# A fused attention and feed-forward kernel: first-pass scores by single PSUM banks, a new order of products, another ending

## The chip, the cores and the metric

The kernel runs on one core of one Trainium2 chip. The metric is the device time of one execution in microseconds (us). Engines are called by the profile's names: PE (TensorE matmul) with PEld (its weight loads), DVE (VectorE), ACT (ScalarE), POOL (GpSimd) and SP (SyncE, which here only issues DMAs). Each runs its own queue in order, and they meet through semaphores.

## The reference

Four sequences of 1024 tokens with 256 features. Every token is normalised, and the result goes through an attention layer (16 query heads, 2 key heads, 16 features a head, rotary positions) and, beside it, through a gated feed-forward layer with a Walsh-Hadamard transform. Both results are added to x.

```python
xn = layernorm(x)
q, k, v = xn @ wq + bq, xn @ wk + bk, xn @ wv + bv     # 16, 2 and 2 heads of 16
q, k = rotate(q) * 16 ** -0.5, rotate(k)
attn = softmax(q @ k.T * 16 ** -0.5)                    # 1024 x 1024 for each head
a = (attn @ v) @ wo + bo
h = fwht(silu(xn @ W1.T) * (xn @ W3.T))                 # 1024 wide
out = x + a + h @ W2.T
```

## The kernel before

**Stages.** There are `NIT` = 8 iterations, one for each sequence and key head, and each has `PERIODS` = 16 periods. Iteration i also carries the feed-forward work of token block i (512 tokens, 8 blocks) and prepares the projections of block i + 2. Products of float32 quality are made of three products of rounded parts (`TERMS`).

**Two passes over the scores.** The exponentials need the row maxima first. The first pass ("S1", one of 64 `UNITS` for each half of an iteration's heads) makes scores with queries on the partitions: two products of 48 rows, which lie in the two row halves of PE (rows 0 to 63 and 64 to 127) and go to the two banks of a slot. DVE takes the maximum over both banks with one `tensor_reduce` of 128x1024 (`unit`, L1295), and the two halves can run in PE side by side. The maxima are turned by DVE, placed by SP among the query rows (`place_maxima`) and so enter the second pass. The second pass (`score`, L1545) makes scores with keys on the partitions, one head into one bank; three banks (4 to 6) take turns, and ACT reads each with an exponential (L1079). `sums` (L1558) multiplies the exponentials by the values into bank 7; a step has four heads, and the trace has eight PE records for it. A period has four units of the first pass, four calls of `scores` (each of two heads, again in the two row halves) and two steps of `sums`.

**The slots.** Banks 0 to 3 are two slots of two banks in the iterations (slots 2 and 3 share banks 4 to 7 and serve the opening). Every entry into a slot waits on `ring_free` until the former entry has been read in full, and its reader waits on `ring_full`. `ring_table` counts these at build time; `PIECES`, `FULLS` and `FREES` say how many pieces, fills and readings an entry has. A unit is one piece, one fill and one reading. The entries of slot 0 are mostly the period's own work: `UP` (eight a block: gate and linear products, 24 products of 512 columns in four pieces, read by ACT's `gate` and `linear` and DVE's `gated`, L1267), `DN` (four a block, 48 products of 256 columns, read by `down`), `WO` (the output projection of a half, read by `projected_sums`), `XT`, `QK`, `Q2` and `VT` (turned tokens, projections and values of block i + 2). First-pass units use slot 1 and, where slot 0 has time, slot 0.

**The order** is written out by hand. `walk_iteration` calls, for each kind of period, `scores`, `first` (a unit), `own` (pieces of the period's entry), `sums_before` (the step left from the period before) and `sums` in the order in which PE has them. `kind_of` names the kind: with a trailing "o" where ACT also copies bank 7 (`save_sums`), `None` where a period has no entry. `LEAD` = 24 units run ahead of the second pass. ACT and DVE have orders of their own for each kind.

**The end.** After the last step of `sums`, `select` moves numerators and denominators of the last heads by two products with a selecting matrix; DVE makes reciprocals of 64x256 and multiplies, and PE makes the output projection of both halves; the last block leaves from ACT's DMA queue.

## Time and profile before

| | us |
|---|---|
| median of 3 runs | 1079.11 (1078.23 to 1080.97) |
| the profiled execution | 1075.6 |
| its span, first to last instruction | 1073.8 |
| PE busy, share of the span | 1014.3, 94% |
| DVE busy | 771.2, 72% |
| ACT busy | 707.5, 66% |
| POOL busy | 347.2, 32% |

The profiled execution lies 3.5 us below the median. A busy PE record reaches from the start of a product to its modelled end, and records overlap: two products that follow each other closely have starts .23 us apart and last .39 us each. So the distance of starts tells how fast PE works, and the busy share tells little about it.

### The profile page before, as it was taken

To read this page: it belongs to the slowest core of one execution; us is meant where nothing else is said; L and a number is where in the kernel's file an instruction comes from. 1 tells how busy PE (TensorE), PEld (TensorE's weight loads), DVE (VectorE), ACT (ScalarE), POOL (GpSimd) and SP (SyncE) were. 2 spreads that over 40 slices of the span, in tenths; PEclk is the share of its full clock that TensorE was granted. 3 is DMA by queue.
4 is the path that set the end of the run, shared out by engine and by line. 5 is a ranking of instruction groups with operands and counts; after the bars stand their busy time and mean duration, and the time that the engine had idled before them with its cause. 6 is when DMAs were issued, how large, how long until landed. Compare 5 with 4: busy or idle time off the path is not lost.

```text
span 1073.8 us, 19578 instructions
## 1 busy us (share of the span) xinstructions
PE 1014.3 (94%) x7604; PEld 549.6 (51%) x7604; DVE 771.2 (72%) x934; ACT 707.5 (66%) x1336; POOL 347.2 (32%) x300
## 2 busy tenths in 40 slices
PE   4889999999999999999999999999999999999997
PEld 3554445545554555545554455545555454644454
DVE  5996688677776778767786777767776778776723
ACT  4256677657765777657776577667775678566873
POOL 5262722073312634054310735126320224012300
PEclk9998999999999999999999999999999999999999
DMA  8762155212052253402242250521123131510001
GB/s 234 177 172 75 53 137 104 74 57 86 17 117 78 76 136 66 100 21 84 64 103 74 97 126 18 117 64 51 51 62 71 33 83 33 111 32 6 12 8 50
DMA packets 64941, 84.03 MB, mean 78 GB/s; under 512 B 19960, under 2 KB 34168, under 8 KB 64848
## 3 DMA queue, kind: packets, MB, share of 16 engines
q1 hardware_dynamic: 63296, 80.74, 29.1%
q10 hardware_dynamic: 1552, 2.03, 0.7%
q8 instruction: 60, 0.98, 0.4%
q14 instruction: 33, 0.27, 0.1%
HBM read 54.97 MB, written 22.51 MB: 72 GB/s over the span
## 4 chain that ended last, share of the span: by engine, by line
PE 66%; DVE 17%; ACT 5%; issue 4%; DMA 4%; SPq 3%; POOL 2%; DVEq 0%; ACTq 0%; POOLq 0%
PE ps L1501 16%; PE ps L1558 14%; PE ps L1545 13%; DVE negpart L1295 11%; PE ps L1456 9%; PE ps L1513 8%; PE ps L1467 3%; DVE hid L1267 3%; PE ps L1434 3%; ACT work L1079 2%; DMA qk_parts<-hid 1%; DMA xn<-in_x 1%; SPq L776 1%; SPq L784 1%; DMA recip_rows<-dens 1%
## 5 line engine op out<-in xcount | busy, mean ns | idle before, releaser
L1295 DVE TENSOR_REDUCE negpart<-ps 128x2 f32<-128x1024 f32 x512 | 619.0, 1224 | 235.7 <-PE ps L1456 234.8
L1079 ACT ACTIVATE work<-ps 128x512 f32<-128x512 f32 x1024 | 560.0, 603 | 262.3 <-PE ps L1545 256.9
L1558 PE MATMUL ps<-work,vb 128*32 128x512 f32 x2048 | 274.6, 609 | 5.8 <-ACT osum L1090 5.0
L1545 PE MATMUL ps<-qh,kb 50*128 50x512 f32 x1024 | 265.1, 450 | 10.3 <-ACT work L1079 7.4
L1456 PE MATMUL ps<-kb,qh 48*128 48x512 f32 x1024 | 226.8, 433 | 9.6 <-DVE negpart L1295 5.3
L1545 PEld LDWEIGHTS ps<-qh,kb 50*128 50x128 f32 x1024 | 123.4, 185 | 212.3 <-ACT work L1079 159.0
L1501 PE MATMUL ps<-xf,w_p 64*128 64x512 f32 x1536 | 218.3, 400 | 7.4 <-DVE negpart L1295 1.4
L1501 PEld LDWEIGHTS ps<-xf,w_p 64*128 64x128 f32 x1536 | 143.6, 185 | 49.7 <-DVE hid L1267 16.3
L933 POOL TENSOR_TENSOR hid_p<-hid,hid_p 128x512 fp32r<-128x512 f32 x64 | 82.2, 1286 | 203.1 <-ACT hid_p L1068 203.1
L1456 PEld LDWEIGHTS ps<-kb,qh 48*128 48x128 f32 x1024 | 98.1, 185 | 82.7 <-DVE negpart L1295 48.4
L1513 PEld LDWEIGHTS ps<-w2t_p,hid_p 64*128 64x128 f32 x1536 | 107.7, 185 | 34.2 <-DVE negpart L1295 27.1
L929 POOL TENSOR_TENSOR hid<-hid 128x512 f32<-128x512 f32 x60 | 77.3, 1288 | 136.1 <-DVE hid L1267 119.1
L1513 PE MATMUL ps<-w2t_p,hid_p 64*128 64x256 f32 x1536 | 116.8, 282 | 2.0
L952 POOL TENSOR_TENSOR attnt<-attnt,recips 128x512 f32<-128x512 f32 x15 | 19.3, 1285 | 282.0 <-DMA recips<-recip_rows 282.0
L1558 PEld LDWEIGHTS ps<-work,vb 128*32 128x32 f32 x2048 | 40.8, 108 | 83.1 <-issue 57.4
L1267 DVE SCALAR_TENSOR_TENSOR hid<-hid,ps 128x512 f32<-128x512 f32 x60 | 40.7, 678 | 5.2 <-ACT hid L1058 5.2
L1068 ACT CAST hid_p<-hid 128x512 fp32r<-128x512 f32 x64 | 40.0, 627 | 0.7 <-POOL hid L929 0.7
L1064 ACT COPY hid<-ps 128x512 f32<-128x512 f32 x60 | 37.1, 618 | 2.2 <-PE ps L1501 2.2
L1434 PE MATMUL ps<-xt,wqkv_p 128*128 128x512 f32 x126 | 36.7, 430 | 1.8 <-DVE xt L1260 1.4
L1467 PE MATMUL ps<-wo_sb,attnt 128*128 128x256 f32 x128 | 36.1, 415 | 1.5 <-DVE attnt L1422 0.9
L1058 ACT ACTIVATE hid<-ps 128x512 f32<-128x512 f32 x60 | 36.7, 611 | 1.2 <-PE ps L1501 0.3
L1275 DVE TENSOR_TENSOR y<-y,ps 128x256 f32<-128x256 f32 x32 | 13.2, 412 | 26.9 <-PE ps L1513 26.9
(125 smaller groups left out, 484.6 us busy)
## 6 DMA issues: line engine op xcount, KB each, us to landing
xf<-xn_parts SPq DMA_DIRECT2D x32, 512.0 KB, 8.5
qh<-qk_parts SPq DMA_DIRECT2D x192, 64.0 KB, 2.3
xn_parts<-xt SPq DMA_DIRECT2D x14, 512.0 KB, 3.5
qh<-mturned SPq DMA_DIRECT2D x256, 2.0 KB
y<-in_x SPq DMA_DIRECT2D x8, 512.0 KB, 4.8
attnt<-osum SPq DMA_DIRECT2D x124, 32.0 KB, 2.0
recips<-recip_rows SPq DMA_DIRECT2D x120, 32.0 KB, 1.8
xn<-in_x SPq DMA_DIRECT2D x7, 512.0 KB, 5.0
```

What stands on the lines that cost most here:

```text
L929: nc.gpsimd.tensor_tensor(hid[1][:, c, :], hid[1][:, c, :], hid[0][:, c, :], ALU.mult).then_inc(hid_done, 1)
L933: nc.gpsimd.tensor_tensor(hid_p[1][:, c, :], hid[1][:, c, :], hid_p[0][:, c, :].bitcast(F32), ALU.subtract).then_inc(hid_lo, 1)
L1079: nc.scalar.activation(prob[(ITSTEPS * i + j) % NPROB][:, h, :], ps[:, 4 + u % 3, :], ACT.Exp, scale=SCALE).then_inc(exp_done, 1)
L1267: nc.vector.scalar_tensor_tensor(at, at, 1.0, two(slot)[:, 0, :], ALU.add, ALU.mult).then_inc(ring_free[slot], 1)
L1295: nc.vector.tensor_reduce(negpart[a][:, f, :, h, t, e], two(slot), AX.X, ALU.max, negate=True).then_inc(ring_free[slot], 1)
L1434: m = pe.matmul(out, left[a], right[b], start=(first and n == 0), stop=(last and n == 2))
L1456: m = pe.matmul(bank[:, r, :], qh[2 * q + f][rows, h, t * P:(t + 1) * P], kb[i % 2][rows, e * 512:(e + 1) * 512], start=True, stop=True)
L1467: m = pe.matmul(bank[:, k // 2, k % 2 * D:(k % 2 + 1) * D], attnt[:, f, k * P:(k + 1) * P], wo_sb[:, i % NG, :], start=True, stop=True)
L1501: m = pe.matmul(bank[:, r, :], w13_p[w][rows, k, c * P:(c + 1) * P], xf[v][rows, k, :], start=(k == 0 and t == 0), stop=(done and t == 2))
L1513: m = pe.matmul(bank[:, r, 0:D], hid_p[w][rows, c, at * P:(at + 1) * P], w2t_p[v][rows, c, :], start=(c == 0 and t == 0), stop=(c == HC - ...
L1545: pe.matmul(ps[:, 4 + u % 3, :], kb[i % 2][rows, kt * P:(kt + 1) * P], qh[2 * a + f][rows, h, :], start=True, stop=True).then_inc(s2_done, 1)
L1558: m = pe.matmul(ps[VW * h:VW * (h + 1), 7, :], vb[b % 2][g][:, kt, :], prob[(ITSTEPS * i + j) % NPROB][:, h, :], start=(kt == 0), stop=(kt ...
```

## The change

1. **Units in two pieces.** `PIECES["S1"]`, `FULLS["S1"]` and `FREES["S1"]` become 2. A piece is one product into one bank, first of the upper row half (bank r = 1), then of the lower. DVE reduces each bank with an instruction of its own (128x512) when that bank is full. Where a unit follows a unit in its slot, a piece waits only until its own bank has been read (`RING[entry][3]`).
2. **A new order.** All kinds in `walk_iteration` are rewritten with `first(slot, n, ...)`, which places single halves; scores or own pieces stand between the two halves of a unit. ACT's order is adapted.
3. **SP's queue.** `load_turned(i + 1)` and `load_queries(i + 1, 1, 0)` now stand behind `spread_recips(i, 0)` and `place_maxima(i + 1, 0, 0)`.
4. **The end.** In the last iteration the four `DN` entries move one period ahead (11 to 14), the last `UP` to period 9, and `WO` of the first half gets period 15 (kind `WOz`). `select` is replaced by `last_values`: DVE turns bank 7 in blocks of 32x32, takes reciprocals of 128x8, multiplies, turns back, and PE adds its products with `wo_last` (rows of `wo` spread out, loaded in iteration 6) to products of the heads that were ready. The two halves of the last addition are 128x512 each as before; the 128x1024 addition is in period 15.
5. **The opening.** In `weights2` two more products stand behind the wait for the stored queries; the kinds `Nos` and `Not` of the first two periods are rewritten too.

In iteration 3, a period of kind `UP` away from ACT's copies, PE's queue before (L1501 is `UP`, L1456 a unit, L1545 scores, L1558 sums):

```order
L1501 MATMUL ps<-xf,w_p 128x512 x12
L1456 MATMUL ps<-kb,qh 128x512 x2
L1545 MATMUL ps<-qh,kb 128x512 x2
L1558 MATMUL ps<-work,vb_1 32x512 x4
L1545 MATMUL ps<-qh,kb 128x512 x2
L1456 MATMUL ps<-kb,qh 128x512 x2
L1501 MATMUL ps<-xf,w_p 128x512 x6
```

The same place after (L1538 is `UP`, L1495 a half of a unit, L1582 scores, L1595 sums):

```order
L1538 MATMUL ps<-xf,w_p 128x512 x6
L1495 MATMUL ps<-kb,qh 128x512
L1538 MATMUL ps<-xf,w_p 128x512 x6
L1495 MATMUL ps<-kb,qh 128x512
L1582 MATMUL ps<-qh,kb 128x512 x2
L1595 MATMUL ps<-work,vb_1 32x512 x4
L1495 MATMUL ps<-kb,qh 128x512
L1582 MATMUL ps<-qh,kb 128x512 x2
L1495 MATMUL ps<-kb,qh 128x512
L1538 MATMUL ps<-xf,w_p 128x512 x12
```

A unit's two products, which stood together, now have six `UP` products or two scores between them.

In iteration 7, period 4 (kind `WOo`), PE's queue before (L1467 is `WO`):

```order
L1558 MATMUL ps<-work,vb_1 32x512 x4
L1456 MATMUL ps<-kb,qh 128x512 x4
L1545 MATMUL ps<-qh,kb 128x512 x4
L1467 MATMUL ps<-wo_sb,attnt 128x256 x4
L1545 MATMUL ps<-qh,kb 128x512 x2
L1558 MATMUL ps<-work,vb_1 32x512 x4
```

and after (L1504 is `WO`):

```order
L1495 MATMUL ps<-kb,qh 128x512
L1582 MATMUL ps<-qh,kb 128x512 x2
L1495 MATMUL ps<-kb,qh 128x512
L1504 MATMUL ps<-wo_sb,attnt 128x256 x4
L1582 MATMUL ps<-qh,kb 128x512 x2
L1495 MATMUL ps<-kb,qh 128x512 x2
L1595 MATMUL ps<-work,vb_1 32x512 x4
L1495 MATMUL ps<-kb,qh 128x512 x2
L1595 MATMUL ps<-work,vb_1 32x512 x4
```

The step left from the period before now stands behind all scores and `WO`, and one unit lies between it and the next step.

The end of DVE's queue before:

```order
L1419 RECIPROCAL qe<-ps 64x256
L1422 TENSOR_TENSOR attnt<-ps,qe 64x256
L1419 RECIPROCAL qe<-ps 64x256
L1422 TENSOR_TENSOR attnt<-ps,qe 64x256
L1340 TENSOR_TENSOR y<-y,ps 128x1024
L1428 TENSOR_TENSOR y<-y,ps 128x512 x2
```

and after:

```order
L1370 TENSOR_TENSOR y<-y,ps 128x1024
L1451 STREAM_TRANSPOSE work<-ps 128x256 x2
L1454 RECIPROCAL work<-work 128x8 x2
L1457 TENSOR_TENSOR work<-work 128x8x16 x2
L1461 STREAM_TRANSPOSE work<-work 128x256 x2
L1465 TENSOR_TENSOR y<-y,ps 128x512 x2
```

The large addition has moved ahead of the last sums, and the two long reciprocals have become eight short instructions.

The core of the diff:

```diff
-PIECES = {"XT": 2, "QK": 4, "Q2": 2, "WO": 4, "UP": 4, "DN": 4, "VT": 1, "S1": 1}
-FULLS = {"XT": 2, "QK": 2}
-FREES = {"XT": 2, "UP": 2, "VT": 2}
+PIECES = {"XT": 2, "QK": 4, "Q2": 2, "WO": 4, "UP": 4, "DN": 4, "VT": 1, "S1": 2}
+FULLS = {"XT": 2, "QK": 2, "S1": 2}
+FREES = {"XT": 2, "UP": 2, "VT": 2, "S1": 2}
...
         elif kind in ("DN", "DNo"):
             scores(0)
-            first(0)
-            first(1)
-            sums_before()
-            own(0)
-            scores(1)
-            first(1)
-            own(1)
+            first(0, 0, 1)
+            first(1, 0, 1)
+            sums_before()
+            scores(1)
+            own(0)
+            first(1, 0)
+            own(1)
+            first(1, 1)
...
         elif kind == "QK":
...
-            own(0)
-            first(1)
-            own(1, 2, 3)
-            first(1)
-            sums(i, 2 * p)
+            own(0, 1, 2)
+            first(1, 0)
             scores(3)
+            first(1, 1)
+            own(3)
             extra()
         elif kind is None:
             scores(0)
-            first(0)
+            first(0, 0, 1)
+            first(1, 0)
             scores(1)
-            first(1)
+            first(1, 1)
             sums_before()
+            first(0, 0)
             scores(2)
-            first(0)
-            first(1)
+            first(0, 1)
+            sums(i, 2 * p)
+            first(1, 0)
             scores(3)
-            sums(i, 2 * p)
+            first(1, 1)
...
-                dve.wait_ge(*filled(("S1", i, a, u)))
...
-                nc.vector.tensor_reduce(negpart[a][:, f, :, h, t, e], two(slot), AX.X, ALU.max,
-                                        negate=True).then_inc(ring_free[slot], 1)
+                for n, r in enumerate((1, 0)):
+                    dve.wait_ge(*filled(("S1", i, a, u), n + 1))
+                    nc.vector.tensor_reduce(negpart[a][:, f, r, h, t, e:e + 1], two(slot)[:, r, :], AX.X, ALU.max,
+                                            negate=True).then_inc(ring_free[slot], 1)
...
-                if k == 0 and RING[entry][2] > 0:
+                if k == 0 and RING[entry][3] > 0:
+                    pe.wait_ge(ring_free[slot], RING[entry][3])
+                if k == 1 and RING[entry][2] > RING[entry][3]:
                     pe.wait_ge(ring_free[slot], RING[entry][2])
```

## Rows read from the trace of the kernel before

**Rows 1.** The page's busy times: engine, us, share of the span, instructions.
```profile
PE 1014.3 (94%) x7604; PEld 549.6 (51%) x7604; DVE 771.2 (72%) x934; ACT 707.5 (66%) x1336; POOL 347.2 (32%) x300
```

**Rows 2.** Timeline, an `UP` period: start, length, engine, line, operation, count, [idle before].
```profile
493.10 1.66 PE L1501 MATMUL ps<-xf,w_p 64*128 64x512 f32 x12
...
496.73 0.87 PE L1501 MATMUL ps<-xf,w_p 64*128 64x512 f32 x6
...
498.37 0.40 PE L1456 MATMUL ps<-kb,qh 48*128 48x512 f32 x2
498.70 1.06 PE L1558 MATMUL ps<-work,vb 128*32 128x512 f32 x8
499.69 0.49 PE L1545 MATMUL ps<-qh,kb 50*128 50x512 f32 x2
500.09 0.49 PE L1456 MATMUL ps<-kb,qh 48*128 48x512 f32 x2
500.69 0.49 PE L1501 MATMUL ps<-xf,w_p 64*128 64x512 f32 x2
```

**Rows 3.** Timeline of DVE, the end of the same period.
```profile
498.81 1.23 DVE L1295 TENSOR_REDUCE negpart<-ps 128x2 f32<-128x1024 f32 x1 [0.54 <-PE ps L1456]
499.95 0.68 DVE L1267 SCALAR_TENSOR_TENSOR hid<-hid,ps 128x512 f32<-128x512 f32 x1
```

**Rows 4.** Timeline of PE, sums and then the first piece of a `DN` entry.
```profile
547.66 1.07 PE L1558 MATMUL ps<-work,vb 128*32 128x512 f32 x8
548.81 0.39 PE L1513 MATMUL ps<-w2t_p,hid_p 64*128 64x256 f32 x2
```

**Rows 5.** Timeline of PE, a `None` period, until the first product of the next.
```profile
891.25 0.50 PE L1545 MATMUL ps<-qh,kb 50*128 50x512 f32 x2
...
892.70 0.49 PE L1545 MATMUL ps<-qh,kb 50*128 50x512 f32 x1 [0.46 <-ACT work L1079]
...
897.94 0.73 PE L1501 MATMUL ps<-xf,w_p 64*128 64x512 f32 x4
```

**Rows 6.** Timeline of PE, the waits of a `WOo` period (iteration 7, period 4).
```profile
975.74 0.73 PE L1456 MATMUL ps<-kb,qh 48*128 48x512 f32 x4 [0.61 <-DVE negpart L1295]
...
977.39 0.49 PE L1545 MATMUL ps<-qh,kb 50*128 50x512 f32 x1 [0.46 <-ACT work L1079]
...
983.04 1.06 PE L1558 MATMUL ps<-work,vb 128*32 128x512 f32 x8 [1.16 <-ACT osum L1090]
```

**Rows 7.** Timeline of PE, iteration 3: start of its period 0, of its first `UP`.
```profile
444.30 0.50 PE L1456 MATMUL ps<-kb,qh 48*128 48x512 f32 x2
...
477.93 1.66 PE L1501 MATMUL ps<-xf,w_p 64*128 64x512 f32 x12 [0.27 <-DVE negpart L1295]
```

**Rows 8.** Timeline of PE, period 11 of the last iteration, scores without units between.
```profile
1028.07 1.48 PE L1545 MATMUL ps<-qh,kb 50*128 50x512 f32 x3 [0.48 <-ACT work L1079]
```

**Rows 9.** Timeline of PE, the end: last sums, last products of the output projection.
```profile
1060.19 1.06 PE L1558 MATMUL ps<-work,vb 128*32 128x512 f32 x8
...
1067.62 1.13 PE L1467 MATMUL ps<-wo_sb,attnt 128*128 128x256 f32 x4 [0.95 <-DVE attnt L1422]
```

**Rows 10.** Timeline of DVE, the end: the last two additions.
```profile
1068.74 1.28 DVE L1428 TENSOR_TENSOR y<-y,ps 128x512 f32<-128x512 f32 x2
```

**Rows 11.** Groups of DVE by line and shape: busy us, mean ns | idle before.
```profile
L1295 DVE TENSOR_REDUCE negpart<-ps 128x2 f32<-128x1024 f32 x512 | 619.0, 1224 | 235.7 <-PE ps L1456 234.8
...
L1318 DVE STREAM_TRANSPOSE mturned<-mparts 128x32 f32<-128x32 f32 x32 | 6.5, 202 | 0.0
L1308 DVE TENSOR_REDUCE negmax<-negpart 128x16 f32<-128x32 f32 x32 | 5.9, 186 | 1.6
...
L1334 DVE RECIPROCAL dens<-dens 128x32 f32<-128x32 f32 x15 | 5.2, 346 | 0.1
L1419 DVE RECIPROCAL qe<-ps 64x256 f32<-64x256 f32 x2 | 3.5, 1758 | 1.9 <-PE ps L1568 1.9
```

**Rows 12.** Stages: start:end, length, busy us (instructions) of the engines, PE clock, DMA.
```profile
77.00:90.60 13.60, 12.87 (x50) 5.24 (x49) 9.66 (x10) 9.57 (x19) 10.48 (x12) 0.50 0.31 100
...
978.10:981.50 3.40, 3.40 (x10) 2.20 (x9) 0.09 (x1) 0.71 (x2) 0.00 (x0) 0.50 0.00 0
```

**Rows 13.** Timeline of PE, the third score of iteration 0.
```profile
75.54 0.50 PE L1545 MATMUL ps<-qh,kb 50*128 50x512 f32 x1 [1.93 <-ACT hid L1138]
```

More of the change, by code:

```diff
@@ L135, in sums_before, with first @@
             sums(i - 1, ITSTEPS - 1)
-    def first(slot):
+    def first(slot, *halves):
         nonlocal unit
-        at = i + unit // (2 * UNITS)
-        if at < NIT:
-            piece(("S1", at, unit // UNITS % 2, unit % UNITS), 0, slot)
-        unit += 1
+        for n in halves:
+            at = i + unit // (2 * UNITS)
+            if at < NIT:
+                piece(("S1", at, unit // UNITS % 2, unit % UNITS), n, slot)
+            unit += n
     def own(*numbers):
@@ L222, in walk_iteration @@
+            first(1, 0)
             scores(3)
+            first(1, 1)
+            own(3)
             extra()
@@ new lines, in walk_iteration @@
+            own(3)
+            scores(3)
+            extra()
+            first(1, 0, 1)
+        elif kind == "UPxo":
+            first(0, 0, 1)
+            first(1, 0)
+            scores(0)
+            first(1, 1)
+            scores(1)
+            own(0)
+            first(1, 0)
+            scores(2)
+            first(1, 1)
+            own(1, 2)
+            scores(3)
+            own(3)
+            first(1, 0, 1)
+            sums_before()
+            extra()
+            sums(i, 2 * p)
+        elif kind == "Nos":
+            first(0, 0)
+            scores(0)
+            first(0, 1)
+            sums_before()
+            scores(1)
+            scores(2)
+            first(0, 0)
+            scores(3)
+            first(0, 1)
+            first(1, 0, 1)
+            sums(i, 2 * p)
+            first(0, 0, 1)
+        elif kind == "Not":
+            first(1, 0)
+            scores(0)
+            first(1, 1)
+            scores(1)
+            first(0, 0)
+            scores(2)
+            first(0, 1)
+            scores(3)
+            first(1, 0, 1)
@@ L342, in walk_opening, with walk_closing @@
         piece(("UP", 0, c), k, 2 + c % 2)
[L345 removed]
+def walk_closing(sums, piece, last_values):
     sums(NIT - 1, ITSTEPS - 1)
[L347 to L350 removed]
+    last_values()
 def ring_table():
[L356 removed]
+    full, free, at, before = [0] * 4, [0] * 4, {}, [None] * 4
     def count(entry, k, slot):
         if k == 0:
[L360 removed]
+            at[entry] = (slot, full[slot], free[slot], free[slot] - (entry[0] == before[slot] == "S1"))
+            before[slot] = entry[0]
             full[slot] += FULLS.get(entry[0], 1)
```

374 lines of the change are left out of this document (179 added, 195 removed).

## The prediction

> **What bounds the kernel now.** I first read the busy times [rows 1]: PE is busy for 94% of the span. That would leave some 60 us to win, and it is misleading. In the timeline the three pairs of one `UP` piece take (0.87 - 0.40) / 2 = 0.235 us from pair to pair [rows 2], while each record lasts 0.39 to 0.40. So a pair that starts 0.5 us after the last still looks busy. I therefore read distances of starts. The costs that I use: a pair (two row halves of 512 columns) 0.235; a step of sums, with the way to the next product, 0.99 (498.70 to 499.69) [rows 2]; the first pair after sums or after a wait takes 0.34 to 0.40 instead (499.69 to 500.09) [rows 2]; the way from a pair into sums 0.33 (498.37 to 498.70) [rows 2].
>
> An `UP` period takes 500.69 - 493.10 = 7.59 us [rows 2]. Its work is 12 `UP` pairs, 4 pairs of scores, 4 units, 2 steps: 20 x 0.235 + 2 x 0.99 + 2 x (0.10 into sums + 0.11 behind them) = 7.1. Only 0.5 is stall: the next `UP` piece starts 0.60 behind the last unit, 0.36 too late [rows 2], because it waits for slot 0, whose last reader, `gated`, runs from 499.95 to 500.63 [rows 3], and the pair behind that wait costs 0.11 more. `gated` itself stood behind a reduce of 1.23 that began at 498.81 [rows 3]. Other kinds have more. The `None` period takes 897.94 - 891.25 = 6.7 us [rows 5] for 8 pairs and 2 steps (about 4.3 us), with PE waiting for exponentials, as three banks take turns. A `WOo` period idles 0.61, 0.46 and 1.16 [rows 6]. The kernel is thus bound by PE's order: who stands in front of which wait. The change is about that.
>
> **The halves on PE.** No product is added. A half alone would waste a row half of PE, so I followed the new order by row halves: always upper, lower, upper, lower (half, scores or `UP` pieces, half). The pairing only shifts by one. I take 0.235 a pair as before.
>
> **The halves on DVE.** 512 reduces of 1224 ns [rows 11] become 1024 of 128x512. Between 186 ns at 32 elements and 1224 at 1024 [rows 11] the slope is 1.05 ns, which makes 0.69 us for 512. Two additions of 128x512 from PSUM take 1.28 together, so the second starts 0.60 behind the first [rows 10]. A unit thus takes 1.20 where one reduce behind another takes about 1.14 (498.81 to 499.95) [rows 3]. That is +0.06 x 512 = 31 us of DVE, which now idles 235.7 us before these reduces [rows 11]; only where DVE gates PE does it cost.
>
> The Trainium skill, VectorE: DVE Perf Modes, section on the TRN2 errata, says that each instruction pays a fixed extra latency, so that many small tiles pay it each time. The slope above agrees with a fixed part of 0.15 us in the length of one. By the rule a unit would cost 1.38; by the row of two additions 0.08 of it overlaps, and my sum uses the row.
>
> **`UP` periods** (59, of which I count 56). Let T be the start of the last `UP` pair. The third unit's halves now start at T + 0.23 and T + 0.47. DVE begins 0.44 behind a unit (498.37 to 498.81) [rows 2, 3], at T + 0.67; two halves, then `gated`: T + 1.87 to T + 2.55; `UP` can start at T + 2.6. PE itself comes there at T + 0.47 + 0.33 + 0.99 + 0.34 + 0.24 = T + 2.36. So the stall shrinks from 0.36 to 0.25 only: the new order does not take it away, DVE's queue is next late. Smaller waits (0.05) go. 0.15 x 56 = **8.4 us**. Bounds: nothing if halves cost 0.69 each, 0.5 x 56 = 28 if `gated` never gates.
>
> **`DN` periods** (28 with units). The first `DN` piece starts 1.15 behind the sums' start instead of 0.99 [rows 4]: it waits for the unit in slot 0. It now stands behind the second scores. 0.16 x 28 = **4.5 us**. Halves of 512 columns between `DN` products of 256 hold one row half up for 0.12, four times a period, two of them new; waits of about 0.2 at units behind scores go. I call that even.
>
> **`None` periods** (6 with units outside the last iteration). Scores no longer stand two pairs in a row; units lie between, and a bank's exponential has its time. Walked through, PE needs 4.7, DVE 4 x 1.20 + small ones = 5.2, so 5.3 instead of 6.7: 1.4 x 6 = **8.4 us**. If exponentials still pace it, 0.5 x 6 = 3.
>
> **`WOo` periods** (4). Of 2.2 us of idle [rows 6] the 1.16 for ACT's copy of bank 7 stays in part: the left-over step ends, 0.6 later its result is there, ACT copies for 0.6, and only a unit (0.6 with its transitions) covers it, so 0.35. Of the rest 0.25 stays. 1.6 x 4 = **6.4 us**.
>
> **Periods 0 to 3 of iterations 1 to 5.** They take 477.93 - 444.30 = 33.6 us [rows 7]. Walking the new order I save some 2 us at scores that stood in fours, but `Q2` now stands right behind `own(3)` of `QK` in the same slot: PE waits for the last `QK` product's end and ACT's reading of it, 0.4 + 0.6 with nothing in between, and the exponentials behind `projected` come later. Left are 0.4 x 5, and 1 in iteration 0: **3 us**.
>
> **The last iteration.** Scores without units stand for exponentials, 0.48 of idle and then 0.49 from one to the next [rows 8]. Filling period 11 with `DN` and 15 with `WO` hides work there: **3 us** (0 to 5).
>
> **The end.** Before: sums end at 1061.25, the last addition at 1068.74 + 1.28 = 1070.02 [rows 9, 10], 8.8 us. After: two transposes of 128x256 at about 0.42 (between 0.20 for 128x32 and 0.68 for 512 elements), two reciprocals of 128x8 at 0.20 (from 346 ns at 32 and 1758 at 256 [rows 11]), two products of 128 elements at 0.28, two transposes, less overlap: 2.5. Then four PE records, 1.13 [rows 9], and one addition 0.68 with 0.14 of hand-over: 4.5. **4.3 us** (3 to 5). The hidden price is `WO` of the first half, which lay under the reciprocals and is now in period 15; that is in the 3 us above.
>
> **The clock.** PE's granted clock was 0.50 of full (1.2 GHz) from 77.00 to 90.60 and from 978.10 to 981.50 [rows 12]. Ahead of both PE had stood: 1.93 us for ACT at 75.54 [rows 13], and the waits of `WOo` [rows 6]. The second should go with these: **1.5 us** (half of the stage). The first wait of 1.93 keeps its cause, ACT's chain; one half-unit before it covers 0.2. I take no gain there; +5 if the clock stays up. DVE, busy in the opening, loses 0.06 x 24 = 1.4, and earlier maxima in SP's queue give about as much back.
>
> **Sum:** 8.4 + 4.5 + 8.4 + 6.4 + 3 + 3 + 4.3 + 1.5 = 39.5. 1075.6 - 39.5 = 1036.1 for the profiled execution; the median stood 3.5 higher: **1040 us**.
>
> **Rivals.**
> - *The pairs break (slower).* Halves shifted by one may lose the weight load that was hidden in an even pair. The price is that of the pair behind a wait, 0.34 - 0.235 = 0.105 us [rows 2]; at both halves of 512 units that is 107 us, less some 20 hidden where PE waits anyway: 1040 + 87 = 1127; at one half in two thirds of the units 1040 + 36 = 1076. It ends slower from 0.04 us for each half on (40 / 1024). For it: no even half-shifted stretch is in the trace. Against: the two row halves start with their own skews and keep 0.235. Chance 0.09, two thirds of it above 1082.
>  The Trainium skill, TensorE: Matmul & The Clock Gate, section The mechanism, says that a weight load overlaps a running product only in another row group. If the trace followed it, even pairs could not run at 0.235, since each loads weights into both halves that run; they do, so the rule bears little weight here.
> - *DVE's fixed cost.* At 1.38 a unit `gated` ends 0.18 later and `UP` gains nothing, `None` is held at 5.9, the opening pays 4 more: 8.4 + 3.6 + 4 = 16 less gain, 1056. Chance 0.14.
> - *Exponentials still pace* `None`, `WOo` and the last iteration: 5 + 4 + 3 + 2 = 14 less, 1054. Chance 0.13.
> - *More goes than I count*: `gated` gates no longer (+15), the clock stays up in the opening (+5): 1020. For it: short reduces let ACT and DVE interleave more finely. Chance 0.16.
> - *The queue of SP takes over* (turned tokens late for the first `UP`): 0.03, near 1060.
> - The forecast itself, 1030 to 1050: 0.45.
>
> **The numbers.** Range 1018 to 1062: it leaves out most of the broken pairs and the far end of the larger gain, some 0.15. What a measurement of this kernel can tell from no change is about 0.3%, 3 us. Faster by more: 0.92; within: 0.02; slower: 0.06.
>
> **What the profile after would show.** DVE's reduces 1024 times near 0.69, two in a row 0.60 apart; an `UP` period of 7.43; `UP` still 0.2 to 0.3 late behind `gated`; `None` near 5.3; one wait of about 1 us before `Q2`, behind ACT's projection; 4.5 us from the last sums to the last addition; no half clock near the end. Wrong would be: pairs 0.34 apart around halves, or `UP` periods without a stall.

## The result, and the profile after

| | before | after |
|---|---|---|
| median, us | 1078.67 (1076.36 to 1080.97, 4 runs) | 1061.84 (1059.16 to 1065.72, 4 runs) |
| profiled execution, us | 1075.6 | 1059.16 |
| its span, us | 1073.8 | 1057.3 |

The ratio is 0.983, 95% interval 0.980 to 0.986: 17 us faster. Forecast were 1040 us and 39.5 us of gain: the time lies at the upper end of the range, and less than half of the gain came. The medians in this document are of all runs, while the ratios leave out runs that lie over 1.5% above the fastest of the same kernel.

The page of the kernel after, busy times, as [rows 1]:

```profile
PE 999.1 (94%) x7608; PEld 550.9 (52%) x7608; DVE 801.8 (76%) x1450; ACT 705.7 (67%) x1335; POOL 346.7 (33%) x299
```

DVE works 30.6 us more (31 forecast), PE's share is what it was. The share again says little. So I compare stage by stage, from the first product that an iteration's order places to that of the next. (The first scores would mislead: before, a unit and eight products that turn tokens stood ahead of an iteration's first score, 1.45 us of work, and 2.4 us of other work in iterations 6 and 7; after, next to nothing does.) For iteration 3 the two ends are, before (PE's timeline; start, length, engine, line, operation, count, [idle before]):

```profile
444.30 0.50 PE L1456 MATMUL ps<-kb,qh 48*128 48x512 f32 x2
...
569.53 0.50 PE L1456 MATMUL ps<-kb,qh 48*128 48x512 f32 x2
569.96 1.09 PE L1473 MATMUL ps<-ident,xn 128*128 128x128 f32 x8
571.35 0.49 PE L1545 MATMUL ps<-qh,kb 50*128 50x512 f32 x2 [0.29 <-DMA qh<-mturned]
```

and after:

```profile
438.13 0.50 PE L1495 MATMUL ps<-kb,qh 48*128 48x512 f32 x1
...
559.11 0.49 PE L1495 MATMUL ps<-kb,qh 48*128 48x512 f32 x1
559.11 0.74 PE L1582 MATMUL ps<-qh,kb 50*128 50x512 f32 x2
```

125.2 us became 121.0. All stages in this way (us; "early load" is experiment 4's second kernel, told of below, whose profiled execution took 1039.82; "last sums" is the start of the last product of the sums):

| stage | before | after | gain | forecast gain | early load |
|---|---|---|---|---|---|
| opening, to iteration 0 | 73.1 | 77.4 | -4.3 | 0 | 72.6 |
| iteration 0 | 120.7 | 117.3 | 3.4 | 7.7 | 117.8 |
| iterations 1 to 5 | 626.5 | 611.0 | 15.5 | 11.2 | 608.3 |
| iteration 6 | 121.1 | 123.5 | -2.4 | 7.8 | 117.9 |
| iteration 7, to the last sums | 119.2 | 120.1 | -0.9 | 8.9 | 113.5 |
| last sums to the end | 13.2 | 7.9 | 5.2 | 4.3 | 7.9 |

The forecast column is the prediction's terms put down to their stages (it adds up to 39.9, since it has all 59 `UP` periods; the term on the clock is in iteration 7). Iterations 6 and 7 contradict it with their sign. The opening does too, and experiment 2 is about that. In iterations 6 and 7 PE waits where it did not before. PE's waits after (engine, line, what for; us in total, times, longest):

```profile
PE ps L1538 <- DMA xf<-xn_parts: 9.9, 2, 5.1
PE ps L1582 <- ACT work L1104: 6.7, 23, 0.5
PE ps L1471 <- ACT qe L1070: 4.2, 6, 0.8
PE ps L1495 <- DVE negpart L1325: 3.7, 4, 1.9
```

The first line is new (before, PE waited for `xf` once, for 1.2 us): `xf` are the turned tokens of the feed-forward part, 4 transfers of 512 KB a block, and the first `UP` of iterations 6 and 7 stands in period 1, not in period 4. PE's timeline in iteration 6:

```profile
813.43 0.60 PE L1595 MATMUL ps<-work,vb 128*32 128x512 f32 x3
819.16 1.22 PE L1538 MATMUL ps<-xf,w_p 64*128 64x512 f32 x4 [5.13 <-DMA xf<-xn_parts]
```

SP's queue tells why. Before, the tokens for iteration 6 (which begins at 820.35) leave at 797.13, ahead of everything that waits for VectorE:

```profile
796.49 0.53 SPq L806 DMA_DIRECT2D dens<-sums_rows  x1
797.13 2.62 SPq L733 DMA_DIRECT2D xf<-xn_parts  x4
...
805.60 0.34 SPq L812 DMA_DIRECT2D recip_rows<-dens  x1
813.05 3.56 SPq L815 DMA_DIRECT2D recips<-recip_rows  x8
816.65 4.41 SPq L784 DMA_DIRECT2D qh<-mturned  x8
```

After, they stand behind the spread of the reciprocals and the maxima, and leave at 805.83, as iteration 6 begins (805.78); the last of the four is issued at 808.95, and PE goes on at 819.16:

```profile
794.92 3.58 SPq L838 DMA_DIRECT2D recips<-recip_rows  x8
798.54 4.41 SPq L807 DMA_DIRECT2D qh<-mturned  x8
803.05 2.67 SPq L799 DMA_DIRECT2D qh<-qk_parts  x6
805.83 3.12 SPq L756 DMA_DIRECT2D xf<-xn_parts  x4
```

The wait costs more than its 5.1 us. Stages of PE around it (start:end, length, busy us of PE, PEld, DVE, ACT, POOL, PE clock, DMA share, GB/s):

```profile
817.00:820.00 3.00, 0.83 (x4) 0.80 (x6) 0.00 (x0) 0.00 (x0) 0.00 (x0) 0.50 1.03 182
820.00:823.80 3.80, 3.80 (x22) 2.09 (x20) 1.39 (x2) 0.85 (x2) 0.00 (x0) 0.50 0.07 10
```

While PE stands, its granted clock falls to 0.50 (1.2 GHz) and stays there for 3.8 us of full work. The same happens in iteration 7 (939.9 to 946.7).

The tokens' new place has a second effect, in iterations 1 to 5. There they leave just ahead of the small transfers that carry the sums' denominators to VectorE. In iteration 4 (which begins at 559.11) the denominators' load leaves SP's queue 15.7 us after that, and with the early load (iteration 4 from 553.43) 9.3 us after, as before the change (9.7 to 10.6):

```profile
574.82 0.33 SPq L829 DMA_DIRECT2D dens<-sums_rows  x1
562.73 0.84 SPq L829 DMA_DIRECT2D dens<-sums_rows  x1
```

VectorE, which never waited for them before, now does, once in each of iterations 1 to 5 and once at the end. With the early load only the wait at the end is left. The first line is the kernel after, the second the early load:

```profile
DVE dens L1364 <- DMA dens<-sums_rows: 15.5, 6, 4.6
DVE dens L1368 <- DMA dens<-sums_rows: 2.0, 1, 2.0
```

The other steps, first an `UP` period, as [rows 2] and [rows 3]. PE, then DVE:

```profile
477.78 0.73 PE L1538 MATMUL ps<-xf,w_p 64*128 64x512 f32 x4
...
482.79 0.39 PE L1495 MATMUL ps<-kb,qh 48*128 48x512 f32 x1
482.79 0.61 PE L1582 MATMUL ps<-qh,kb 50*128 50x512 f32 x2
483.02 0.39 PE L1495 MATMUL ps<-kb,qh 48*128 48x512 f32 x1
...
484.34 0.73 PE L1582 MATMUL ps<-qh,kb 50*128 50x512 f32 x2
484.68 0.39 PE L1495 MATMUL ps<-kb,qh 48*128 48x512 f32 x1
485.15 1.20 PE L1538 MATMUL ps<-xf,w_p 64*128 64x512 f32 x7
```

```profile
483.21 1.29 DVE L1325 TENSOR_REDUCE negpart<-ps 128x1 f32<-128x512 f32 x2 [0.56 <-PE ps L1495]
484.42 0.68 DVE L1296 SCALAR_TENSOR_TENSOR hid<-hid,ps 128x512 f32<-128x512 f32 x1
```

The period takes 485.15 - 477.78 = 7.37 us (7.59 before), and `UP` still starts 0.47 behind the last half, 0.24 late, because `gated` ends at 485.10. VectorE's groups, as [rows 11]:

```profile
L1325 DVE TENSOR_REDUCE negpart<-ps 128x1 f32<-128x512 f32 x1024 | 656.8, 683 | 178.3 <-PE ps L1495 170.9
```

And the end, as [rows 9] and [rows 10], PE and then DVE:

```profile
1047.20 2.78 PE L1595 MATMUL ps<-work,vb 128*32 128x512 f32 x24
```

```profile
1050.05 0.78 DVE L1451 STREAM_TRANSPOSE work<-ps 128x256 f32<-128x256 f32 x2 [1.95 <-PE ps L1595]
...
1051.36 0.76 DVE L1461 STREAM_TRANSPOSE work<-work 128x256 f32<-128x256 f32 x2
...
1053.94 0.69 DVE L1465 TENSOR_TENSOR y<-y,ps 128x512 f32<-128x512 f32 x1 [0.18 <-PE ps L1610]
```

From the sums' end (1049.98) to the last addition's (1054.63) are 4.65 us, 4.5 forecast.

### The profile page after: what moved, and what is told of

It reads as the page before. It is cut to its first block, busy times and chain, and to the rows that moved or that the text cites. A ratio compares the mean times of both kernels' runs of the same rounds, so it can differ in the third digit from the quotient of the medians.

```text
span 1057.3 us, 20100 instructions
## 1 busy us (share of the span) xinstructions
PE 999.1 (94%) x7608; PEld 550.9 (52%) x7608; DVE 801.8 (76%) x1450; ACT 705.7 (67%) x1335; POOL 346.7 (33%) x299
## 4 chain that ended last, share of the span: by engine, by line
PE 64%; DVE 14%; DMA 10%; SPq 7%; ACT 3%; issue 2%; POOL 1%; POOLq 0%; ACTq 0%; DVEq 0%
PE ps L1538 17%; PE ps L1595 14%; PE ps L1495 11%; PE ps L1582 9%; DVE negpart L1325 9%; PE ps L1550 7%; DMA sums_rows<-osum 3%; DVE hid L1296 3%; PE ps L1504 2%; DMA xf<-xn_parts 2%; SPq L799 2%; SPq L838 2%; SPq L807 2%; DMA dens<-sums_rows 1%; ACT work L1104 1%
## 5 line engine op out<-in xcount | busy, mean ns | idle before, releaser
L1325 DVE TENSOR_REDUCE negpart<-ps 128x1 f32<-128x512 f32 x1024 | 656.8, 683 | 178.3 <-PE ps L1495 170.9
L1104 ACT ACTIVATE work<-ps 128x512 f32<-128x512 f32 x1024 | 554.0, 607 | 255.4 <-PE ps L1582 255.0
L1495 PE MATMUL ps<-kb,qh 48*128 48x512 f32 x1024 | 352.4, 434 | 5.8 <-DVE negpart L1325 3.7
L1582 PE MATMUL ps<-qh,kb 50*128 50x512 f32 x1024 | 316.1, 443 | 9.7 <-ACT work L1104 6.7
L1595 PE MATMUL ps<-work,vb 128*32 128x512 f32 x2048 | 272.9, 610 | 1.5 <-DVE negpart L1325 1.0
L1495 PEld LDWEIGHTS ps<-kb,qh 48*128 48x128 f32 x1024 | 164.4, 188 | 181.4 <-DVE negpart L1325 139.7
L1538 PE MATMUL ps<-xf,w_p 64*128 64x512 f32 x1536 | 229.4, 406 | 14.2 <-DMA xf<-xn_parts 9.9
L1582 PEld LDWEIGHTS ps<-qh,kb 50*128 50x128 f32 x1024 | 142.3, 186 | 109.4 <-ACT work L1104 89.2
L1538 PEld LDWEIGHTS ps<-xf,w_p 64*128 64x128 f32 x1536 | 155.8, 189 | 60.4 <-DVE hid L1296 18.9
L1595 PEld LDWEIGHTS ps<-work,vb 128*32 128x32 f32 x2048 | 41.7, 108 | 91.2 <-issue 72.7
L1083 ACT ACTIVATE hid<-ps 128x512 f32<-128x512 f32 x60 | 35.8, 597 | 9.0 <-PE ps L1538 8.7
L1504 PE MATMUL ps<-wo_sb,attnt 128*128 128x256 f32 x120 | 32.6, 408 | 2.2 <-POOL attnt L979 2.2
L1471 PEld LDWEIGHTS ps<-xt,wqkv_p 128*128 128x128 f32 x126 | 23.4, 199 | 17.6 <-ACT qe L1070 6.7
```

The lines of the kernel that those rows point to most:

```text
L1104: nc.scalar.activation(prob[(ITSTEPS * i + j) % NPROB][:, h, :], ps[:, 4 + u % 3, :], ACT.Exp, scale=SCALE).then_inc(exp_done, 1)
L1325: nc.vector.tensor_reduce(negpart[a][:, f, r, h, t, e:e + 1], two(slot)[:, r, :], AX.X, ALU.max, negate=True).then_inc(ring_free[slot], 1)
L1471: m = pe.matmul(out, left[a], right[b], start=(first and n == 0), stop=(last and n == 2))
L1495: m = pe.matmul(bank[:, r, :], qh[2 * q + f][rows, h, t * P:(t + 1) * P], kb[i % 2][rows, e * 512:(e + 1) * 512], start=True, stop=True)
L1504: m = pe.matmul(bank[:, k // 2, k % 2 * D:(k % 2 + 1) * D], attnt[:, f, k * P:(k + 1) * P], wo_sb[:, i % NG, :], start=True, stop=True)
L1538: m = pe.matmul(bank[:, r, :], w13_p[w][rows, k, c * P:(c + 1) * P], xf[v][rows, k, :], start=(k == 0 and t == 0), stop=(done and t == 2))
```

## Experiments

Each kernel's ratio is to the kernel before, run on the same chip. "After" below is the changed kernel. Where the length of a period is given here, it goes from the period's first score to the next period's first score, which compares kernels of the same order.

**1. SP's old order under the new one.** The kernel after, with the two calls back at their old places:

```diff
+                if after:
+                    load_turned(i + 1)
+                    load_queries(i + 1, 1, 0)
                 spread_recips(i, 0)
                 if after:
                     place_maxima(i + 1, 0, 0)
-                    load_queries(i + 1, 1, 0)
-                    load_turned(i + 1)
                     load_queries(i + 1, 1, 1)
```

> The changed kernel with one part undone: SP's queue in the order of before (turned tokens and the queries of the first half ahead of the spread reciprocals and the maxima). Theory: the missed gain is mostly PE's wait for the turned tokens at the first UP of iterations 6 and 7 (period 0 took 16.5 and 16.1 us against 8.5), because their four transfers are now issued only at the start of the iteration. Then period 0 of iterations 6 and 7 falls to 8 to 9 us, PE no longer waits for xf, and the time is about 1062 - 15 = 1047. The odd 11.4 us of period 2 in iteration 4 should go as well. Rival: period 0 is long because the left-over step of sums stands behind everything in the new order, so that the sums leave late; then it stays near 15 us and the time near 1060.

Measured: 1084.94 us (1076.2 to 1100.99, 10 runs), ratio 1.001, interval 0.997 to 1.005. This theory fell. The wait for `xf` is gone, but PE's first wait is another:

```profile
PE ps L1583 <- DMA qh<-mturned: 22.1, 7, 4.0
```

The maxima now reach `qh` late at the turn of every iteration: period 15 takes 10.0 to 11.7 us (7.24 after), period 0 7.8 to 9.2 (6.2 after). In SP's waits the small transfer ahead of them is what became slow, with 2 MB of tokens just sent off:

```profile
SPq L838 <- DMA recip_rows<-dens: 66.6, 15, 8.7
```

against, in the kernel after:

```profile
SPq L838 <- DMA recip_rows<-dens: 23.3, 15, 3.0
```

The kernel before, with the same order in SP's queue, has 53.9 us there (longest 7.1). It could afford that: its first score came 1.45 us behind the start of the iteration, and PE waited for the maxima once, for 0.29 us at 571.35. The new order wants them at once. So the move in SP's queue is needed in seven changes of iteration. PE pays for it with waits for the tokens before the two iterations whose first `UP` comes in period 1, and in the others VectorE waits for the denominators. The edit moves six loads of queries (64 KB each) together with the tokens; the two were not tried apart.

**2. The opening.** The kernel after, with the wait for the stored queries two places later in `weights2`:

```diff
-                if n == W2HEAD - 10:
+                if n == W2HEAD - 8:
```

> The changed kernel with the wait inside the opening's weight products put back by two products (eight behind it, not ten). Theory: the half clock from 45.6 to 59.3 us, which before did not have, comes of the two short stands of PE ahead of it (1.1 us each instead of one of 1.9) and goes away: the first score starts near 73.5 to 75 instead of 77.7, the whole 3 us faster, 1059. Rival: the opening is paced by DVE's 48 half reduces (0.06 us for each unit) and not by the clock; then the first score stays near 77 and the time near 1062.

Measured: 1059.94 us (1056.52 to 1065.83), ratio 0.982, interval 0.977 to 0.987: no difference from the kernel after (0.983). The first score came at 74.5, but kernels that share the opening of the kernel after had it at 72.1 to 77.7, and those with the old opening at 73.1 to 79.0. Over all traces the late ones are those with 13.6 us or more at half clock between 43 and 63 us (77.1 to 79.0); with none or 3.4 us the first score comes at 72.1 to 74.5. The 4.3 us lost in the opening are thus not shown to come from any step of the change.

**3. Single parts.** First, on the kernel before, the halves alone: units in two pieces, each pair of halves placed together as before, two reduces.

```diff
-            piece(("S1", at, unit // UNITS % 2, unit % UNITS), 0, slot)
+            for n in range(2):
+                piece(("S1", at, unit // UNITS % 2, unit % UNITS), n, slot)
```

> The kernel before with the halves alone: a unit is two pieces and two reduces, each bank is freed by itself, but the halves stand together where the unit stood, and every order, queue and ending is that of before. Theory: the finer release of banks is worth little by itself: gated still stands behind the third unit, DVE has 0.06 us more for each unit; an UP period falls from 7.59 to about 7.45, None from 6.7 to about 6.2, the opening loses 1 to 2; together -6 to -12 us, 1069. Rival: the order brings all and the halves cost: 1080 or more.

Measured: 1087.53 us (1084.35 to 1090.56, 10 runs), ratio 1.006, interval 1.004 to 1.008: slower. `UP` takes 7.65 instead of 7.59, `DN` 7.58 instead of 7.45. An `UP` period pays 0.06 us, which is what a unit costs VectorE more where two reduces follow each other.

Then the move in SP's queue alone, on the kernel before:

> The kernel before with the new order of SP's queue alone. What the run with the old queue showed (19 us lost, PE waiting 22 us for the maxima at seven iteration starts, in a kernel whose iterations are 4 us shorter) can mean two things. Theory: the maxima are late only because PE comes to them sooner; in the slower kernel of before they were just in time (one wait of 0.3 us), so moving them wins nothing here and the late turned tokens cost 5 us in each of iterations 6 and 7: about 1079 + 8 = 1087. Rival: moving them wins by itself (in iterations 4 and 5 one period was 0.4 and 1.2 us longer): 1077 or less.

Measured: 1092.38 us (1090.9 to 1097.93), ratio 1.011, interval 1.008 to 1.014. Iterations 1 to 5 are unchanged (125.2 to 126.2 from first score to first score), period 0 of iterations 6 and 7 takes 14.07 and 12.70 instead of 8.49, each with a stage at half clock behind it:

```profile
PE ps L1500 <- DMA xf<-xn_parts: 6.5, 2, 3.9
```

And, on the kernel after, the new order with one 128x1024 reduce for both halves, which frees the slot as a whole:

```diff
-                for n, r in enumerate((1, 0)):
-                    dve.wait_ge(*filled(("S1", i, a, u), n + 1))
-                    nc.vector.tensor_reduce(negpart[a][:, f, r, h, t, e:e + 1], two(slot)[:, r, :], AX.X, ALU.max,
-                                            negate=True).then_inc(ring_free[slot], 1)
+                dve.wait_ge(*filled(("S1", i, a, u), 2))
+                nc.vector.tensor_reduce(negpart[a][:, f, :, h, t, e], two(slot), AX.X, ALU.max,
+                                        negate=True).then_inc(ring_free[slot], 1)
```

> The changed kernel with whole units on DVE: the new order of products and halves of PE as it is, but one reduce of 128x1024 behind both halves, and a slot is freed as a whole. Theory: with slot 1 alone in UP periods a unit now spans up to 1 us on PE (six UP products between its halves) and then 1.23 on DVE before the next may start, so PE waits at units: UP periods of 8 to 9 us, the time 1100 or more. The new order needs the halves. Rival: the order alone brings the gain and the halves on DVE only cost their 0.06 each: 1050 to 1060.

Measured: 1188.67 us (1184.93 to 1189.37), ratio 1.099, interval 1.094 to 1.103. `UP` takes 8.78, `DN` 8.86, and

```profile
PE ps L1494 <- DVE negpart L1324: 92.9, 181, 1.3
```

Neither the halves nor SP's order gains alone. The new order needs banks that come free one by one and, by experiment 1, SP's new order, and that one needs the two late iterations looked after.

**4. The tokens early where they are needed early.** The kernel after, with the load ahead of the third part of the sums, before the last two iterations only:

```diff
                 place_maxima(i, 1, 1)
+                early = after and i + 3 >= NBLK
+                if early:
+                    load_turned(i + 1)
                 move_sums(i, 2)
...
                     load_queries(i + 1, 1, 0)
-                    load_turned(i + 1)
+                    if not early:
+                        load_turned(i + 1)
```

> The changed kernel, but at the change to iterations 6 and 7 the turned tokens are sent off ahead of the third move of sums (end of period 11) instead of behind the maxima (end of period 15). Theory: the wait for them (9.9 us in the profile, 5.1 and 4.8, with half clock behind each) goes, the maxima stay in time: period 0 of iterations 6 and 7 falls from 16.5 and 16.1 to 11 to 12, the time from 1062 to about 1052. Rival: the 2 MB then run ahead of the small transfers of the sums and maxima, which come late instead: period 15 or 0 grows by as much, the time stays near 1060.

Measured: 1042.68 us (1038.62 to 1047.72), ratio 0.964, interval 0.960 to 0.968. The tokens leave at 774.82 instead of 805.83:

```profile
774.82 2.61 SPq L756 DMA_DIRECT2D xf<-xn_parts  x4
```

The waits for `xf` fall from 9.9 to 0.2 us, iteration 6 from 123.5 to 117.9, iteration 7 from 120.1 to 113.5, and there is no half clock behind period 0. And in every iteration (`early = after`):

> The same early place for the turned tokens in all iterations. Theory: where nobody waits for them soon (first UP in period 4) an early start only crowds the transfers of sums and maxima at the end of the iteration; but it frees the start of the next one, where sums and reciprocals are now slowed in some iterations (period 2 or 3 up to 3.6 us longer). I expect these to cancel within 5 us of the run that moves them for iterations 6 and 7 alone: 1047 to 1057. Rival: transfers collide as in the run with the old queue: 1070 or more.

Measured: 1044.04 us (1037.63 to 1051.94), ratio 0.967, interval 0.960 to 0.973, the same within the intervals. The traces do differ: iterations 1 to 5 take 608.3 us against 614.8 with the tokens early in two iterations only, where VectorE still waits 15.6 us for the denominators. Two of its four runs lie at 1038 to 1040 with a mean granted clock of 0.991 and 0.988, two at 1048 to 1052 with 0.977 and 0.974.

**5. What is left in the projections.** `Q2` waits 0.7 us six times for ACT. The kernel after, with all `QK` pieces ahead of the last unit and scores:

```diff
-            own(0, 1, 2)
+            own(0, 1, 2, 3)
             first(1, 0)
             scores(3)
             first(1, 1)
-            own(3)
             extra()
```

> The changed kernel with the last QK piece one place ahead, so that a unit and two scores stand between it and Q2. Theory: in QK periods PE stands 0.94 us between the last QK product and Q2 (1.17 from start to start instead of 0.23), for ACT's reading of the slot; with 0.6 us of cover period 1 falls from 10.7 to about 10.1 in six iterations, 3 to 4 us in all. Rival: the scores that are now behind it are paced by exponentials anyway and the wait moves there: under 1 us.

Measured: 1064.24 us (1059.76 to 1065.24), ratio 0.983, interval 0.980 to 0.986, no gain. `QK` grew from 10.71 to 11.29, and the wait doubled:

```profile
PE ps L1470 <- ACT qe L1069: 8.1, 6, 1.6
```

ACT's copy stands behind exponentials 6 to 8 in its queue, and their scores now come later. So both engines together, on the kernel of experiment 4 (the copy moves ahead of those exponentials):

```diff
                         exponentials(i, j, 0, 6)
                         projected(i + 2, 0)
-                        exponentials(i, j, 6, 8)
                         projected(i + 2, 1)
+                        exponentials(i, j, 6, 8)
                         projected(i + 2, 2)
```

> The kernel with the early load of the last two iterations, and the QK period mended on both engines: all four projection pieces ahead of the unit and the last scores, Q2 behind them, and ACT's second projection ahead of its exponentials 6 to 8. Theory A (Q2 waits for ACT's projection, 0.7 us six times, and only the order of ACT spoilt the attempt on PE alone): QK 10.7 to about 10.0, six times, 4 us: 1038. Theory B (exponentials then late by one action at the next XT-like start, which gives the gain back): no change, 1042, with ACT waits at the scores of the period behind.

Measured: 1044.68 us (1043.41 to 1047.9), ratio 0.967, interval 0.965 to 0.969: nothing against experiment 4. The wait is gone and `QK` takes 9.85, as theory A says, but `WO` behind it takes 8.4 to 13.4. The longest is in iteration 4, DVE's timeline:

```profile
576.66 0.35 DVE L1367 RECIPROCAL dens<-dens 128x32 f32<-128x32 f32 x1 [4.54 <-DMA dens<-sums_rows]
```

VectorE stands for the denominators' transfer, and PE's units behind it. This kernel, like that of experiment 4 on which it is built, still sends the tokens of iterations 1 to 5 off just ahead of that transfer. So the reciprocals one unit later:

```diff
                         units(i, u, 1)
+                        if kind == "WO":
+                            reciprocals(i - 1, 1)
                         units(i, u + 1, 1)
...
-                    if p == 1 and i > 0:
+                    if p == 1 and i > 0 and kind != "QK":
```

> The kernel with the early load and the mended QK periods, and VectorE takes the reciprocals of the denominators one unit later, in the WO period instead of at the end of the QK period. In the trace without this step VectorE stands up to 4.5 us (iteration 4) for the denominators' transfer, 12.9 us over the execution, its units stand behind that, and the WO period takes 9.9 to 13.4 us where it has taken 7.75 in others. Theory A (the transfer's fixed arrival gives back what QK gained): with a unit ahead of the wait, VectorE stands at least 0.9 us less in each of five iterations, XT to WOx falls from 35.8 us on average to about 35: 1041. Theory B (the reciprocals then hold up their own transfers, POOL's normalising and the second output projection): WOx grows by what WO gives, no change, 1045.

Measured: 1057.32 us (1054.9 to 1071.29), ratio 0.978, interval 0.973 to 0.982: some 12 us slower than the kernel without this step, more than theory B has it. `WO` does take 7.75 in four of five iterations, but `WOx` 12.5 to 15.5 (9.3 before this step), with

```profile
PE ps L1510 <- POOL attnt L982: 10.2, 5, 3.1
```

That is, PE now reaches the second output projection before its normalised sums are there, and behind the wait stands half clock. In iteration 1 PE waits 1.67 us at 216.10, and then:

```profile
217.00:226.40 9.40, 9.40 (x33) 3.55 (x32) 5.00 (x7) 3.16 (x6) 9.02 (x10) 0.51 0.02 4
```

The chain from the last sums over the denominators, the reciprocals and POOL to that projection bounds these periods here, and what PE saves ahead of it comes back as a wait, with half clock on top. Its length is not fixed, though: POOL's product starts 24.2 to 27.3 us after the iteration's start in the two kernels of this experiment with the mended `QK`, but 21.9 to 23.2 with the early load in all iterations, where the second output projection begins at 25.4 at the earliest. The mended `QK` together with that load was never run, so what it would bring is open.

**6. `WOo` and everything together.** The kernel of experiment 4, where in `WOo` the left-over sums stand right behind the second scores:

```diff
             scores(1)
+            sums_before()
             first(1, 0)
...
             first(1, 0, 1)
-            sums_before()
-            first(0, 0, 1)
             sums(i, 2 * p)
+            first(0, 0, 1)
```

> The kernel with the early load of the last two iterations, and in a WOo period the sums of the period before put right behind the second pair of scores, so that ACT's copy of bank 7 is done before the sums of this period. Four WOo periods remain (periods 0 and 4 of iterations 6 and 7: 10.07, 11.54, 10.06, 9.99 us in the trace of the early load). Theory A (the copy is what these periods wait for): each 0.5 to 1 shorter, together 2 to 4 us: about 1039. Theory B (it is DVE's 1024-column addition and the output transfers): no change, 1042.

Measured: 1047.41 us (1044.19 to 1048.62), ratio 0.970, interval 0.968 to 0.971: some 0.5% slower than experiment 4, though the intervals touch. Period 0 of iterations 6 and 7 grew from 10.07 and 10.06 to 11.59 and 11.39: the unit in slot 0 now stands last, with no sums to cover its reduces, and the next `UP` needs that slot. PE waits for it:

```profile
927.10 1.28 PE L1556 MATMUL ps<-xf,w_p 64*128 64x512 f32 x7 [1.61 <-DVE negpart L1343]
```

Neither theory had that.

> All of it together: early load in the last two iterations, WOo with the sums placed early, QK mended on both engines, and the wait for the feed-forward weights two places later in the opening. If the gains add: 1042.7 - 3 - 4 - 0 = about 1036; if neither of the two edits does anything, 1042.

Measured: 1055.51 us (1052.99 to 1056.05), ratio 0.976, interval 0.975 to 0.978. Iterations 1 to 5 gain nothing, as in experiment 5, and iterations 6 and 7 lose as in the kernel above. In the trace 55.8 us of the span are at half clock, against 32.0 in experiment 4's, 30.7 of them between 43 and 95 us, in the opening and behind it. Whether the later weight wait has a part in that is open: the same edit alone (experiment 2) had a first score at 74.5, this kernel at 77.1. The best kernel stays that of experiment 4.

## Why the prediction was wrong, point by point

**The step that failed** is the one on SP's queue, in the part on the clock: "earlier maxima in SP's queue give about as much back". It priced the move by what was put ahead and forgot the transfers that were put behind. Of the queue that the tokens were moved past I read only the gain, not when the tokens are wanted: period 4 in iterations 1 to 5, but period 1 in iterations 6 and 7. The rows for it were there before: the issue at 797.13 for a first `UP` at 829.61, with some 20 us to spare, and between the old place and the new the waits for VectorE's reciprocals and maxima. The rival *The queue of SP takes over* described this, gave 1060 and got a chance of 0.03. Experiment 4 brings only those tokens forward and comes to 1042.7; the move alone on the kernel before (experiment 3) costs 1.1%. Of the 19 us between the medians of the kernel after and of experiment 4, the stages show 12.2 in iterations 6 and 7. The rest is not put down to a cause: the profiled executions differ by 3.9 us in the opening, and the mean granted clock by 0.978 to 0.985.

**`UP`:** right. Forecast 7.43 with 0.25 of stall behind `gated`, measured 7.37 to 7.40 with 0.24.

**Halves on PE:** right. A half and a score share a pair at 482.79, and the next such pair starts 0.23 later. The 0.34 from 484.34 to 484.68 is that of the first pair behind sums, as before. The rival *pairs break* is out.

**Halves on DVE:** right. 683 ns, and 1.29 for two in a row, so 0.60 apart. The Trainium skill, VectorE: DVE Perf Modes, section on the TRN2 errata, has many small tiles pay a fixed latency each, by which I had put a unit at 1.38. It says that of operands in SBUF, and these reduces read PSUM, for which its table has a fixed term too. In 0.683 such a part is there, and 0.08 of it overlaps with the reduce before. The rival of the fixed cost is out.

**`DN`:** sized too small. Counted by PE's order, from the first product of period 12 to the next iteration's first, the four periods took 31.1 in iterations 1 to 5 and take 29.6: 1.5 an iteration against 0.64 forecast. I counted the wait at the first `DN` piece only, and had called the other waits even. (From score to score period 15 goes from 8.92 to 7.24, but that is mostly the work that stood ahead of the next iteration's first score: by PE's order it goes from 7.47 to 7.23.)

**`None`:** 8.4 forecast, 4.0 came, and the fault is in the time before. My 6.7 was counted from 891.25, which is the last pair of scores of the period ahead; the period's own first score is at 891.86:

```profile
891.86 0.39 PE L1545 MATMUL ps<-qh,kb 50*128 50x512 f32 x1
...
897.94 1.67 PE L1501 MATMUL ps<-xf,w_p 64*128 64x512 f32 x12
```

That is 6.08, and the six took 5.9 on average. The same period after takes 887.00 - 881.88 = 5.12, and the six 5.2, about the 5.3 forecast:

```profile
881.88 0.99 PE L1582 MATMUL ps<-qh,kb 50*128 50x512 f32 x2
...
887.00 0.86 PE L1538 MATMUL ps<-xf,w_p 64*128 64x512 f32 x6
```

That PE needs only 4.7 is not shown. The first scores still start 0.49 apart there, so exponentials pace a part of the period, as that rival has it.

**Periods 0 to 3 of iterations 1 to 5:** sized too small, 0.4 an iteration forecast. By PE's order they took 33.6 [rows 7]. They take 32.3 in iteration 3 of the kernel after and in iterations 1 to 3 with the early load, where no half clock falls in them, and up to 35.9 elsewhere. The wait of `Q2` (0.78 at 453.47) came as forecast. What I had not listed is the denominators' transfer, late behind the tokens. In iteration 4 of the kernel after VectorE waits 4.6 us for it and PE for VectorE, and `WO` takes 11.40 instead of 7.75, with 3.4 us of half clock:

```profile
579.82 0.50 PE L1495 MATMUL ps<-kb,qh 48*128 48x512 f32 x1 [1.93 <-DVE negpart L1325]
```

**`WOo`:** sized too large, 1.6 for each of four forecast. Where no half clock falls in (iteration 6 before, iteration 7 with the early load), the stretch from the start of period 0 to that of period 5 goes from 41.5 to 39.5, and 0.6 of that belongs to `UP`: 0.7 for each `WOo`. In the kernel after period 4 still shows 0.67 of wait for a reduce at 844.01, and the early load has half clock in period 4 of iteration 6, which takes 1.5 back.

**The last iteration and the end:** 7.3 forecast, and 1.6 + 5.2 came. Periods 9 to 15 of iteration 7 went from 46.6 to 45.1. From the sums' end to the last addition's the gain is 4.1 (4.3 forecast), and another 1.1 lies behind the last addition, which I had not counted and no run explains.

**The clock:** forecast 1.5 of gain, came a loss. The stage near 978 is gone, as forecast, but others came: the span of before has 20.6 us at half clock, that of after 45.8. PE was busy for 16.3 and 39.5 us of these, so an estimate of what its products took longer is half of the difference, 11.6. 13.6 us of the stages lie in and behind the two waits for `xf`.

Summed up: some terms came larger and some smaller than put down, and 35.8 of 39.5 us are there in the profiled execution of the early load everywhere. The two medians with early tokens, 1042.7 and 1044.0, lie 3 to 4 us above the forecast of 1040; that this is so near is in part luck, since `None` and `WOo` fell short by what `DN` and the first periods brought more. What put the forecast wrong was one edit that I had costed at nothing.

## What to carry to other kernels

When a step is moved in a queue, look up for each use of it when it is wanted, the earliest one first: here two of eight iterations wanted the tokens in period 1 and not in period 4, and the move that the new order needs everywhere cost 12 us in these two. Then look at what is issued behind the new place. Here 2 MB of tokens lengthened the small transfers behind them wherever they stood: those of the reciprocals at the old place, those of the denominators at the new one, neither at the early one. A stall taken away ahead of a chain of transfers returns at its end as long as the chain arrives as late as before, so measure that chain first, and what lengthens it. And when two orders are compared, cut the timeline at the first product of a stage and not at a landmark that may have moved within it.

## What the runs showed of the hardware

**The granted clock goes with much of the spread.** The early load everywhere took 1037.63, 1039.82, 1048.25 and 1051.94 us at mean granted clocks of 0.991, 0.988, 0.977 and 0.974. Multiplied, time by clock, that is 1028, 1027, 1024 and 1025. The kernel after gives 1036 to 1040 so, the kernel of the reciprocals 1025 to 1032, no more than experiment 4's (1031 to 1034). The product overstates the clock's part, since half clock under a wait costs nothing, so that all of that kernel's loss is the clock's is suggested by it and not shown.

**Waits and half clock go together in these traces**: 1.67 us of waiting on POOL stood ahead of 9.4 us at 0.51, 5.13 on `xf` around 6.8 at 0.50. Where `WO` took 7.75 it ran at full clock; in the profiled execution of experiment 4 a stage of 3.4 us at half clock falls in period 2 of each of iterations 1 to 4 (`WO` 9.4 to 10.5), in that of the early load everywhere in iterations 4 and 5 only (9.4 there, 7.75 in 1 to 3). VectorE's wait for the denominators does not decide it: with experiment 4's kernel it is there in iteration 5 too (2.4 us) without such a stage, and with the early load everywhere it is absent in iterations 4 and 5. Which short wait starts such a stage was not settled by any run.

**Large transfers delay small ones behind them.** SP's wait for the write of 16 KB of reciprocals is 53.9 and 66.6 us over the execution (longest 7.1 and 8.7) in the two kernels that send 2 MB of tokens, and queries, just ahead of it, and 22.1 and 23.3 (longest 2.8 and 3.0) with the early load and in the kernel after.
